# First attention's probabilities transposed in pairs of 64-row tiles, in a new order of the unit

## The reference, cut to what matters

```
x = x + attn(layernorm(x));  in attn:
q = einsum('ahe,bce->bach', W_Q, x);  k, v likewise
scores = einsum('bach,baCh->bacC', k, q)            # row c of k against all C of q
masked = where(tril(ones(512, 512)), scores, -1e10)
probs  = softmax(masked / 8, axis=-1)
z      = einsum('bacC,baCh->bach', probs, v)
out    = einsum('aeh,bach->bce', W_O, z)
```

## Time and profile before

| | us |
|---|---|
| median of 3 runs | 1153.77 (1152.77 to 1156.58) |
| profiled execution, its own time | 1154.38 |
| its span | 1152.6 |
| TensorE busy | 1124.3 (98%) |
| VectorE busy | 790.9 (69%) |
| ScalarE busy | 691.6 (60%) |
| GpSimd busy | 610.0 (53%) |

### The profile page before, as it was taken

The page is one execution under the profiler, slowest core; times in us unless marked ns, Lnnn a source line. Parts: engine busy times, 40 slices in busy tenths (PEclk is TensorE's granted clock), DMA queues, the critical chain, the costliest instruction groups (busy, mean ns, idle before and its releaser), DMA issues.

```text
span 1152.6 us, 20639 instructions
## 1 busy us (share of the span) xinstructions
PE 1124.3 (98%) x7114; PEld 874.4 (76%) x7114; DVE 790.9 (69%) x2417; ACT 691.6 (60%) x1712; POOL 610.0 (53%) x641
## 2 busy tenths in 40 slices
PE   8999999999999999999999999999999999999997
PEld 6777777777777766767667887877878878787676
DVE  6867677667767356778897677768667686675553
ACT  3668677777767224453676647657656566575832
POOL 1456666666664322049896446557465474573330
PEclk9999999999999999999999999999999999999999
DMA  7003333323210401030040001200002100001010
GB/s 255 1 2 132 100 109 113 123 93 123 89 71 2 164 19 55 1 112 22 19 176 1 2 1 36 94 1 1 1 19 99 55 1 1 1 32 42 19 38 18
DMA packets 30310, 64.72 MB, mean 56 GB/s; under 512 B 3840, under 2 KB 16256, under 8 KB 29696
## 3 DMA queue, kind: packets, MB, share of 16 engines
q1 hardware_dynamic: 30208, 63.41, 15.7%
HBM read 41.04 MB, written 22.36 MB: 55 GB/s over the span
## 4 chain that ended last, share of the span: by engine, by line
PE 90%; DVE 4%; POOL 2%; ACT 2%; issue 1%; DMA 0%; DVEq 0%; ACTq 0%; POOLq 0%
PE psum L1532 48%; PE psum L1633 7%; PE psum L1598 6%; PE psum L1615 6%; PE psum L1765 5%; PE psum L1814 5%; PE psum L1799 4%; PE psum L1781 4%; PE psum L1747 2%; PE psum L1827 1%; PE psum L1838 1%; PE psum L1721 1%; POOL rn L780 1%; PE psum L1829 0%; DVE y L1091 0%
## 5 line engine op out<-in xcount | busy, mean ns | idle before, releaser
L735 POOL TENSOR_TENSOR probs<-probs,rden 128x128 f32<-128x128 f32 (+3 forms) x256 | 177.6, 725 | 80.6 <-DVE rden L1149 80.6
L974 ACT ACTIVATE lp<-lp,lneg,rn 128x256 f32<-128x256 f32 (+1 forms) x256 | 143.6, 568 | 11.6 <-DVE lneg L1366 11.5
L890 ACT ACTIVATE probs<-probs,negmax 128x128 f32<-128x128 f32 (+3 forms) x256 | 139.9, 553 | 5.8 <-DVE negmax L1144 5.8
L1134 DVE CUSTOM_DVE_ANT_0 probs<-psum,causal 128x128 f32<-128x128 f32 (+3 forms) x256 | 110.3, 487 | 19.4 <-PE psum L1598 19.3
L768 POOL TENSOR_TENSOR lp<-lp,lrden 128x128 f32<-128x128 f32 x64 | 25.6, 400 | 165.8 <-DVE lrden L1371 165.8
L780 POOL TENSOR_TENSOR rn<-ssm,neg_half 128x8 f32<-128x8 f32 x64 | 108.4, 1693 | 0.0
L1354 DVE CUSTOM_DVE_ANT_0 lp<-psum,local 128x256 f32<-128x256 f32 (+1 forms) x256 | 84.2, 385 | 20.6 <-PE psum L1765 20.6
L771 POOL TENSOR_TENSOR lp<-lp,lrden 128x768 f32<-128x768 f32 x64 | 93.9, 1467 | 0.0
L1532 PE MATMUL psum<-wqkv_hi,hT_lo 128*128 128x512 f32 x192 | 82.0, 427 | 0.1
L961 ACT ACTIVATE sq<-psum 128x512 f32<-128x512 f32 x64 | 38.0, 594 | 68.9 <-PE psum L1532 68.9
L1633 PE MATMUL psum<-pT,v 128*64 128x256 f32 (+3 forms) x512 | 77.7, 446 | 1.4 <-DVE pT L1158 1.0
(11 more groups left out here) (172 smaller groups left out, 3146.7 us busy)
## 6 DMA issues: line engine op xcount, KB each, us to landing
w_raw<-in_w_all SPq DMA_DIRECT2D x22, 380.0 KB, 3.1
w_scratch<-w_half SPq DMA_DIRECT2D x22, 380.0 KB, 2.3
w_scratch<-w_rest SPq DMA_DIRECT2D x22, 380.0 KB, 3.0
x<-in_x SPq DMA_DIRECT2D x8, 512.0 KB, 7.4
aw<-in_w_quads SPq DMA_DIRECT2D x4, 768.0 KB, 5.5
wqkv_lo<-w_scratch SPq DMA_DIRECT2D x6, 512.0 KB, 6.3
wqkv_hi<-w_scratch SPq DMA_DIRECT2D x6, 512.0 KB, 4.5
w_hi<-w_scratch SPq DMA_DIRECT2D x2, 1364.0 KB, 6.5
```

What stands on the lines that cost most here:

```text
L735: ins = pool.tensor_tensor(pr, pr, rden[:, u % 2, h, i:i + 1].broadcast_to([P, TRI[i]]), ALU.mult)
L890: ins = act.activation(pr, pr, ACT.Exp, bias=negmax[:, u % 2, h, i:i + 1], scale=ADH ** -0.5, accum_out=den[:, u % 2, h, i:i + 1])
L974: ins = act.activation(pr, pr, ACT.Exp, bias=lneg[:, u % 2, h, w:w + 1], scale=rn[:, m % 2, w, 0, 2 * j + h:2 * j + h + 1], accum_out=lden ...
L1134: ins = dve.tensor_tensor_reduce(probs[:, u % 2, h, TRI_AT[i]:TRI_AT[i + 1]], bank[:, at:at + TRI[i]], causal[:, S - TRI[i]:S], 1.0, -3e38 ...
```

## The change

The transposes of a block of 128 by 128 become two, of its rows 0 to 63 and 64 to 127, with 64 columns each, into two banks. The 20 blocks are in three groups of 8, 8 and 4 (`T_BLOCKS`): head 0's key blocks 0, 1 and 3, head 1's, and both heads' block 2. A group fills two banks, one for each row half; the copies to `pT` put halves of 64 columns side by side (`transposed`). Copies are as many and as large as before.

A unit's order on TensorE was sA (tiles 3 and 2) of u+2, z of u, sB (tiles 1 and 0) of u+2, pv of u+2, pk and pq of u+3, the six groups t of u+1. It is now pv of u+2, t0 and t1 of u, sA of u+2 (tile 3), t2 of u, sB of u+2 (tiles 2, 1 and 0), z of u, pk and pq of u+3. Tiles 1 and 0 go to banks 4 and 5, and z takes banks 6 and 7 in turn with pv, pk and pq. ScalarE's e0 of u+2 becomes the last item of a unit's list, ahead of the copies of the next unit's transposes; e1 of u+1 follows those. VectorE waits for t2 of unit u before it writes scores of unit u+2 to the same buffer. START and ENTRY are written anew in the same manner; in START ScalarE takes both heads' exponentials of unit 0 before k of unit 1, in ENTRY z.31 comes before kv.0.

```diff
-S_PARTS = {"sA": (0, 1), "sB": (2,)}
-S_BANKS = ((0, 1), (2, 3), (0, 1))
-T_BANKS = (4, 5, 2, 3, 4, 5)
-Z_BANK = 4
+S_PARTS = {"sA": (0,), "sB": (1, 2)}
+S_BANKS = ((0, 1), (2, 3), (4, 5))
+T_BANKS = ((4, 5), (2, 3), (4, 5))
-T_TILES = ((0,), (1, 3), (2,))
+T_BLOCKS = (((0, 0), (0, 1), (0, 3)), ((1, 0), (1, 1), (1, 3)), ((0, 2), (1, 2)))
...
-        START_PE = ("xT.0 pk.0 xT.1 pq.0 pv.0 sA.0 sB.0 pk.1 pq.1 pv.1 sA.1 xT.2 sB.1 pk.2 pq.2 t.0.0 t.0.2 "
-                    "t.0.1 t.0.3 t.0.4 t.0.5 pv.2 sA.2 z.0 pq.3 sB.2 xT.3 pk.3 t.1.0 t.1.1 t.1.2 t.1.3 t.1.4 "
-                    "t.1.5")
+        START_PE = ("xT.0 pk.0 xT.1 pq.0 pv.0 sA.0 sB.0 pk.1 pq.1 pv.1 sA.1 sB.1 xT.2 pk.2 pq.2 t.0.0 t.0.1 "
+                    "pv.2 sA.2 t.0.2 sB.2 z.0 xT.3 pk.3 pq.3")
...
+        START_ACT = ("xT.0 aw.0.0 aw.0.1 aw.0.2 pk.0 xT.1 pq.0 pv.0 e.0.0 e.0.1 pk.1 pq.1 pv.1 xT.2 pk.2 pq.2 "
+                     "t.0.1 t.0.3 e.1.0 t.0.5 e.1.1 pv.2 xT.3 pk.3 e.2.0 pq.3")
...
-        UNIT_PE = ("sA@2 z sB@2 pv@2 pk@3 pq@3 t0@1 t1@1 t2@1 t3@1 t4@1 t5@1")
-        UNIT_DVE = ("sA@2 r0@1 z sB@2 r1@1 aw2@2 pk@3 aw0@3 t0@1 pq@3 aw1@3 t2@1 t4@1")
-        UNIT_ACT = ("e0@1 e1@1 pv@2 aw2@2 pk@3 aw0@3 pq@3 aw1@3 t1@1 t3@1 part@1 t5@1")
+        UNIT_PE = ("pv@2 t0 t1 sA@2 t2 sB@2 z pk@3 pq@3")
+        UNIT_DVE = ("t0 t2 r0@1 t4 sA@2 sB@2 r1@1 z pk@3 aw0@3 aw2@2 pq@3 aw1@3")
+        UNIT_ACT = ("t1 t3 t5 e1@1 pv@2 aw2@2 pk@3 aw0@3 part@1 pq@3 aw1@3 e0@2")
...
-        ENTRY_PE = ("sA.30 z.28 sB.30 pv.30 pk.31 pq.31 t.29.0 t.29.1 t.29.2 t.29.3 t.29.4 t.29.5 sA.31 z.29 "
-                    "sB.31 pv.31 t.30.0 t.30.1 t.30.2 t.30.3 t.30.4 t.30.5 z.30 awo.0 t.31.0 t.31.1 t.31.3 "
-                    "t.31.2 t.31.5 t.31.4 kv.0 z.31 awo.1 x1T.0 KV.0 xq.0 kv.1 awo.2 x1T.1 xq.1 kv.2 KV.1 "
+        ENTRY_PE = ("t.29.0 t.29.1 sA.31 t.29.2 sB.31 z.29 pv.31 t.30.0 t.30.1 t.30.2 z.30 awo.0 t.31.0 "
+                    "t.31.1 t.31.2 z.31 kv.0 awo.1 x1T.0 KV.0 xq.0 kv.1 awo.2 x1T.1 xq.1 kv.2 KV.1 x1T.2 "
...
+        ENTRY_DVE = ("t.29.0 t.29.2 t.29.4 sA.31 r.30.0 sB.31 r.30.1 z.29 t.30.0 t.30.2 t.30.4 z.30 tab.0 "
+                     "r.31.0 tab.1 r.31.1 awo.0 t.31.0 t.31.2 t.31.4 z.31 kv.0 norm2.0 keys.0 awo.1 xq.0 KV.0 "
...
+        ENTRY_ACT = ("t.29.1 t.29.3 t.29.5 e.30.1 pv.31 e.31.0 t.30.1 t.30.3 t.30.5 e.31.1 t.31.1 t.31.3 "
...
             if what == "t":
-                take((what, *at), T_BANKS[at[1]])
+                for half in range(2):
+                    take((what, at[0], 2 * at[1] + half), T_BANKS[at[1]][half])
             if what == "z":
-                take((what, *at), Z_BANK)
+                turn((what, *at), "p")
...
+        def transposed(bank, n):
+
+            g, half = divmod(n, 2)
+            if g < 2:
+                dst = pT[:, g, 0:KEYB_AT[2]].rearrange("p (b s q) -> p b s q", s=2, q=HP)[:, :, half, :]
+                return bank[:, :].rearrange("p (b q) -> p b q", q=HP), dst
+            dst = pT[:, :, KEYB_AT[2]:TRI_AT[T]].rearrange("p h (b s q) -> p h b s q", s=2, q=HP)[:, :, :, half, :]
+            return bank[:, 0:2 * LOC // 2].rearrange("p (h b q) -> p h b q", h=2, q=HP), dst
...
+                if u >= 2 and part == "sA":
+                    for n in (4, 5):
+                        wait_full(dve, plan["t", u - 2, n])
...
-            def transposes(u, n):
+            def transposes(u, g):
...
+                pe.wait_ge(s_prob, 2 * u + (1 if g == 0 else 2))
+                uses = [plan["t", u, 2 * g + half] for half in range(2)]
+                banks_of = [wait_free(pe, use) for use in uses]
+                blocks = [(h, i, c) for h, c in T_BLOCKS[g] for i in range(c, T)]
+                for n, (h, i, c) in enumerate(blocks):
+                    lo = TRI_AT[i] + c * P
+                    for half in range(2):
+                        rows = slice(half * HP, (half + 1) * HP)
+                        ins = pe.transpose(banks_of[half][:, n * HP:(n + 1) * HP], probs[rows, u % 2, h, lo:lo + P],
+                                           ident[rows, rows])
+                        if n == len(blocks) - 1:
+                            ins.then_inc(full[uses[half][0]], 1)
```

More of the change, by code:

```diff
@@ L15 @@
 P = 128
+HP = P // 2
 B, S, D = 4, 512, 256
@@ L312, in unit_at @@
             return c, j, j // 2, 2 * c + j % 2
-        START_PE = ("xT.0 pk.0 xT.1 pq.0 pv.0 sA.0 sB.0 pk.1 pq.1 pv.1 sA.1 xT.2 sB.1 pk.2 pq.2 t.0.0 t.0.2 "
-                    "t.0.1 t.0.3 t.0.4 t.0.5 pv.2 sA.2 z.0 pq.3 sB.2 xT.3 pk.3 t.1.0 t.1.1 t.1.2 t.1.3 t.1.4 "
-                    "t.1.5")
-        START_DVE = ("xs.0 xn.0 xs.1 xT.0 aw.0.0 xn.1 aw.0.1 aw.0.2 pk.0 pq.0 xT.1 sA.0 sB.0 xs.2 pk.1 pq.1 "
-                     "xn.2 r.0.0 sA.1 r.0.1 sB.1 xT.2 pk.2 t.0.0 xs.3 pq.2 t.0.2 t.0.4 xn.3 r.1.0 sA.2 r.1.1 "
-                     "z.0 sB.2 xT.3 t.1.0 pk.3 pq.3 t.1.2 t.1.4")
@@ L322, in build @@
-        START_ACT = ("aw.0.0 aw.0.1 xT.0 aw.0.2 pk.0 pq.0 xT.1 pv.0 e.0.0 pk.1 pq.1 pv.1 e.0.1 xT.2 pk.2 pq.2 "
-                     "t.0.1 t.0.3 t.0.5 pv.2 e.1.0 e.1.1 xT.3 pk.3 pq.3 t.1.1 t.1.3 t.1.5")
+        START_PE = ("xT.0 pk.0 xT.1 pq.0 pv.0 sA.0 sB.0 pk.1 pq.1 pv.1 sA.1 sB.1 xT.2 pk.2 pq.2 t.0.0 t.0.1 "
+                    "pv.2 sA.2 t.0.2 sB.2 z.0 xT.3 pk.3 pq.3")
+        START_DVE = ("xs.0 xn.0 xT.0 aw.0.0 aw.0.1 aw.0.2 xs.1 xn.1 pk.0 xT.1 pq.0 sA.0 sB.0 xs.2 xn.2 pk.1 "
+                     "pq.1 sA.1 r.0.0 r.0.1 sB.1 xs.3 xT.2 pk.2 pq.2 t.0.0 xn.3 t.0.2 t.0.4 sA.2 r.1.0 sB.2 "
+                     "r.1.1 z.0 xT.3 pk.3 pq.3")
@@ L328, in build @@
+        UNIT_DVE = ("t0 t2 r0@1 t4 sA@2 sB@2 r1@1 z pk@3 aw0@3 aw2@2 pq@3 aw1@3")
+        UNIT_ACT = ("t1 t3 t5 e1@1 pv@2 aw2@2 pk@3 aw0@3 part@1 pq@3 aw1@3 e0@2")
         UNIT_POOL = ("f0@1 f1@1 part@1")
-        ENTRY_PE = ("sA.30 z.28 sB.30 pv.30 pk.31 pq.31 t.29.0 t.29.1 t.29.2 t.29.3 t.29.4 t.29.5 sA.31 z.29 "
[9 rows of a table removed]
-        ENTRY_DVE = ("sA.30 r.29.0 z.28 sB.30 r.29.1 pk.31 t.29.0 t.29.2 pq.31 t.29.4 sA.31 r.30.0 z.29 sB.31 "
[8 rows of a table removed]
-        ENTRY_ACT = ("e.29.0 e.29.1 pv.30 pk.31 pq.31 t.29.1 t.29.3 t.29.5 e.30.0 e.30.1 e.31.0 pv.31 t.30.1 "
[7 rows of a table removed]
@@ L356, in build @@
-        ENTRY_POOL = ("f.29.0 f.29.1 f.30.0 f.30.1 f.31.0 f.31.1 norm2.0 norm2.1 kvs.0 norm2.2 kvs.1 y.0 "
[4 rows of a table removed]
+        ENTRY_PE = ("t.29.0 t.29.1 sA.31 t.29.2 sB.31 z.29 pv.31 t.30.0 t.30.1 t.30.2 z.30 awo.0 t.31.0 "
[7 rows of a table added]
+        ENTRY_DVE = ("t.29.0 t.29.2 t.29.4 sA.31 r.30.0 sB.31 r.30.1 z.29 t.30.0 t.30.2 t.30.4 z.30 tab.0 "
[7 rows of a table added]
+        ENTRY_ACT = ("t.29.1 t.29.3 t.29.5 e.30.1 pv.31 e.31.0 t.30.1 t.30.3 t.30.5 e.31.1 t.31.1 t.31.3 "
[7 rows of a table added]
+        ENTRY_POOL = ("f.30.0 f.30.1 f.31.0 f.31.1 norm2.0 norm2.1 kvs.0 norm2.2 kvs.1 y.0 norm2.3 zeros.0 "
[4 rows of a table added]
@@ L894, in evac_pT @@
             def evac_pT(u, n):
-                h, k = divmod(n, 3)
                 use = plan["t", u, n]
[L898 to L901, removed]
+                src, dst = transposed(wait_full(act, use), n)
+                copy(dst, src).then_inc(read[use[0]], 1)
             def evac_x1T(b):
@@ L1151, in evac_pT @@
             def evac_pT(u, n):
-                h, k = divmod(n, 3)
                 use = plan["t", u, n]
-                bank = wait_full(dve, use)
-                at = KEYB_AT[T_TILES[k][0]]
-                w = sum(KEYB[j] for j in T_TILES[k])
-                dve.tensor_copy(pT[:, h, at:at + w], bank[:, 0:w]).then_inc(read[use[0]], 1)
+                src, dst = transposed(wait_full(dve, use), n)
+                dve.tensor_copy(dst, src).then_inc(read[use[0]], 1)
             def evac_z(u):
@@ L1602, in scores @@
                         at += TRI[i]
-            def transposes(u, n):
-                h, k = divmod(n, 3)
-                if k == 0:
-                    pe.wait_ge(s_prob, 2 * u + (h + 1))
-                use = plan["t", u, n]
-                bank = wait_free(pe, use)
-                at = 0
-                for c in T_TILES[k]:
-                    for i in range(c, T):
-                        lo = TRI_AT[i] + c * P
-                        ins = pe.transpose(bank[:, at:at + P], probs[:, u % 2, h, lo:lo + P], ident[:, :])
-                        at += P
-                ins.then_inc(full[use[0]], 1)
+            def transposes(u, g):
[11 more added lines that the diff above has]
+                            ins.then_inc(full[uses[half][0]], 1)
             def weighted_values(u):
```

## The result

The changed kernel takes 1157.47 us (median of 20 runs, 1152.86 to 1160.89); the kernel before took 1152.55 in the same comparison (20 runs, 1149.48 to 1156.58). The ratio is 1.0041, 95% interval 1.003 to 1.0051: slower by 4.9 us, where 1140.4 was forecast. The profiled execution took 1158.8, span 1157.0.

A forecast was written before the change was run, and what follows sets the result against it. TensorE's own work was taken to bound the kernel, ScalarE's round the changed one. Steady -14.7, start +2, end -0.7 sum to -13.4; from 1154.4, less 0.6 for profiled against median time, 1140.4 us; range 1131 to 1151.

The forecast's parts named there:

- e0: First head's exponentials, two units on, in ScalarE's queue: take 2.18 us, hold ScalarE till 2.88 after q's end, delaying copies.
- the start: Before the steady units: the wait at 28.65 ends some 2 us later; +2 us, between 0 and +4.
- TensorE's round: A steady unit on TensorE: 10.14 us of work plus a 0.27 wait ahead of v, 10.41.
- the end: Last units and entry: about 1.5 less, last transposes 0.9 shorter, last values waiting about 1.7; -0.7 us, between -4 and +3.
- The pair: In the units' transposes: two half-row transposes take 0.064 us against 0.109 for a whole one; 20 pairs, 1.28.
- Rival B: In the transposes: a pair costs as much as one full transpose, 0.109 us; kernel 1160 us; chance 0.11.
- rival D: In the transposes: a pair is cheaper but not half, 0.085 us; kernel 1145.5 to 1150 us; chance 0.18.
- Changes of shape: On TensorE: each array shape change costs about 0.19 us, three a unit instead of four.
- ScalarE's round: In steady units: q's rounding, exponentials and copies delay tile 2's scores to 4.08 us after q; unit 10.63.
- Rival C: In steady units: the exponential does not hold back the copies, TensorE's 10.41 us decides; kernel 1132 us; chance 0.13.
- The quads' ends: Three steady units round a quad's weights on ScalarE, 0.3 and 0.5 us longer each; 2.4 back.
- E: In the units: extra waits starve TensorE until its clock falls in each; kernel 1190 us; chance 0.03.

The follow-up runs named there:

- g3: g2 with ScalarE doing the first head's exponential ahead of q's rounding, and the partial sums' work ahead of W's: 1146.01 us (0.9944 to the kernel before).
- g2: g1 with W_a2's remainder ahead of k's remainder on VectorE, in two units a quad: 1145.12 us (0.9932 to the kernel before).
- a2: Changed kernel with the exponential of unit 0's second head put back behind k, q and v of unit 1 on ScalarE: 1157.81 us.
- e3: Changed kernel with cross attention's first keys and values again ahead of the last unit's values, and its first transposes' copy ahead of the output projection's adds: 1151.41 us.
- a3: Changed kernel with the transposed input of batch 2 again ahead of unit 1's scores of tiles 1 and 0: 1153.31 us.
- a1: Changed kernel with batch 1's statistics and normalization again ahead of the first quad's weight remainders, two weights rounded earlier on ScalarE: 1154.66 us.
- a4: Changed kernel with the three start edits of a1, a2 and a3 together: 1154.41 us.
- e2: a4 with batch 2's normalization also put back behind k and q of unit 1 on VectorE: 1151.40 us.
- g1: Changed kernel with six orders put back, the four of the start (e2) and the two of the entry (e3): 1147.41 us (0.9944 to the kernel before).

## Why the prediction was wrong, by its steps

The forecast was -13.4 and the windows show +4.4. Of the 17.8 between them 7.6 lie in the start, 6.0 in the units, 3.0 in the end and 1.2 behind it. Three terms failed: the start, which priced one of three waits and no clock; TensorE's round, which put the seams between transposes and scores at nothing; and the end, which left out the adds ahead of a copy.

**The pair.** Right: 16 pairs from 215.16 to 216.18, 0.064 each. Rival B (0.109) and rival D (0.085) fall; D's unit of 10.83 came true, but not by its price of a pair. The Trainium skill ("TensorE: Matmul & The Clock Gate", section "LDWEIGHTS (loading the stationary operand)") gives a load's time by its columns, whatever its rows: an estimated 107 ns for 128 columns in either half. The trace disagrees: 64 ns for a pair with two such loads.

**Changes of shape.** Here a term failed. I costed nothing between transposes of 64 rows and scores of 64 rows, "all have the same shape". The rows show a seam there all the same: the first pair of scores takes 0.32 (216.18 to 216.50) and the next 0.22; tile 3 is 0.78 instead of 0.70, the third group 0.37 instead of 0.26, tile 2 0.64 instead of 0.54, tiles 1 and 0 with their gap 0.91 instead of 0.79. Together 0.41 a unit. The last 0.12 are no such seam: no transposes stand ahead of tile 1, whose first pair takes 0.20 all the same (217.97 to 218.17), and no run shows why. The third group takes as long in g3 (0.39), where ScalarE has done its copies well before, so the 0.37 needs no wait for them to explain it. TensorE's work in a unit is 297.57 / 28 = 10.63, not 10.14; with the wait of 0.17 ahead of v (0.27 predicted) its round is 10.8, where 10.41 was forecast. That the forecast's unit is 10.63 too is chance.

**ScalarE's round.** Its queue ran as drawn: from q's rounding (213.46) to the scores of tile 2 (217.33) are 3.87, predicted 4.08 - 0.20 = 3.88 (the terms given add up to 4.06), with e0 of 2.18 between. But the wait of 0.2 for its copy, which was to set the pace, is not in the trace: the copies end at 217.19, and TensorE, with its seams, is not ready much before. In g3 ScalarE's round is out of the way and the unit stays at 10.83. So TensorE's own round sets the pace or ties, and the agreement of 3.87 is partly luck. Rival C, TensorE's round, had the mechanism but with 10.41 the wrong size.

**The quads' ends.** 2.4 predicted; the traces show units of 11.59 and 11.36 in place of 10.83, three times: 3.9. The first is ScalarE's weights, as predicted: it rounds them around q's copy, and TensorE's third transposes then wait 0.58 for its copies (194.75). The second, where v waits 0.69 for W_a2's remainder behind k's on VectorE, I had not followed; g2 took it away for 1.6 us in the windows.

**Steady units:** -8.7 in the windows where -14.7 was forecast. 0.20 a unit (5.6) and 1.5 at the quads' ends make 7.1 of a miss of 6.0; against them stand 0.9 that the kernel before has beyond 28 units of 11.24 (315.63 against 314.72).

**Start.** This step failed most: +9.6 where +2 stood, between 0 and +4. The one wait that I followed came as drawn: 2.03, 1.08 from the wait ahead of it and the exponential's 2.17 are 5.28, measured 5.41, and "4 to 5" was said. Three moves I had not priced. The statistics of batch 1 behind W's remainders made a wait of 2.60; x^T 2, in banks that the scores of tiles 1 and 0 now take, one of 1.88; and xn.2, with its wait for GpSimd, ends as late as the exponential, so that putting back the exponential alone gave nothing (a2). And "I leave the start's clock as it is" was wrong: 0.89 over 64.66 us is 7.1 us of full clock lost, against 1.7 before. In the trace 6.1 of the 9.6 are idle time of TensorE and 3.5 longer work.

**End.** The stretch to the output projection, -1.3, is the -1.5 forecast. t.31 and z.31 were not: "waits about 1.7" was the price of z.31 ahead of kv.0, and the adds of awo.0 ahead of t.31.0's copy were not looked at. By the trace the adds make the wait of 2.54, z.31's own wait is 0.80, and it takes 1.37 more at the lower clock. This stretch is +3.6 in the windows where +0.8 was forecast, and e3 gained 6.1; e3 puts both moves back at once, so their shares are not separated.

**Cover by the clock.** The last +1.2, where the change edits nothing, goes with the clock (0.99 for 1.00). The range's slow side took in waits but no lower clock in the start or behind the units, and E looked for its fall in the units, where it stayed at 1.00. Nor do the waits alone fix it: behind the same waits of about 0.54 and 0.89 z.30 took 2.37 or 2.38 in a3, e3 and g2 and 3.93 to 4.53 in a1, a2, a4, e2, g3 and the changed kernel's trace.

What stays open: the shares of the waits and of the clock in the time of the runs, since none has the one without the other; the loss of full clock that remains in g1 and g2 (6.9 and 6.3 beside 4.0 and 3.6); and the start of g2, still 2.5 longer than before (57.60 against 55.07).

## What to carry to other kernels

An order rewritten for the loop is rewritten for its start and its end too: price each item moved there as if it were an edit of its own, since here 10 us hung on six places outside the loop (g1), and the loop gained 8.7. Ask of every reordered queue what waits at its head for another engine (xn.2 for GpSimd's root) and who stands behind it. A wait can have two causes that end together, and then an experiment on one shows nothing (a2): read the trace for what comes next. A halved instruction pays only with an order that can use it, and an order may cost without it: 11.13, 11.90 and 10.83 from 11.24.

## What the runs showed of the hardware that was not expected

- A pair of fp32 transposes of 64 rows in the two halves of the array takes 0.064 us where one transpose of 128 rows takes 0.109; each has a weight load of its own (1280 loads).
- Transposes and products of one shape (64 rows by 128 columns) in turn still cost about 0.1 us at a seam: the first pair of products 0.32, the next 0.22.
- The run-to-run spread of these kernels, some 8 us, follows the granted clock: 0.72 to 0.83 us for each us of full clock lost (correlation 0.97 to 0.98). Values at the lower clock were seen behind waits: z.31 took 3.74 to 4.54 in the six traces in which 2.54 to 2.56 stand ahead of the transposes before it, and 2.37 or 2.38 in the five with 0.33. Behind the shorter waits of z.30 both were seen.
